# Graph network with experts on one core: one-hot rows two groups ahead, a tile's work in another order

## What is computed

```python
h = feats * rsqrt(deg_out)[:, None]
m = segment_sum(h[src], dst, num_segments=n) * rsqrt(deg_in)[:, None]
x = (m @ W_gc + b_gc) + (feats @ W_res + b_res)
logits = x @ Wg + bg
vals, idx = top_k(logits, 2)              # 64 experts, H = 512, gelu between w1 and w2
core = sum of the gated outputs of a node's two experts
y = x + core
y = (y - mean) * rsqrt(var + eps) * gamma + beta      # over the nodes
out = layernorm(feats + y)                # over the features
```

## Time and profile before

| | |
|---|---|
| three runs | 2939.91, 2944.16, 2950.51 us; median 2944.16 |
| profiled execution | 2947.52 us, its span 2945.7 us |
| busy, of the span | PE 2071.2 us (70%), PE weight loads 1711.2 (58%), DVE 1234.2 (42%), ACT 410.9 (14%), POOL 1890.4 (64%) |
| chain that ended last | POOL 40%, PE 25%, issue 19%, DVE 7%, DMA 4%, DVE's sequencer 3% |
| mean granted clock of PE | 0.83 of full speed |

### The profile page before, as it was taken

How to read it: one execution, slowest core, us unless ns; L and a number is a source line. 1 busy time by engine, 2 the same in 40 slices (tenths; PEclk the granted TensorE clock), 3 DMA queues, 4 the chain that set the end, 5 groups by cost and what they waited for, 6 DMA issues and landing times.

```text
span 2945.7 us, 44174 instructions
## 1 busy us (share of the span) xinstructions
PE 2071.2 (70%) x10250; PEld 1711.2 (58%) x10251; DVE 1234.2 (42%) x3115; ACT 410.9 (14%) x1358; POOL 1890.4 (64%) x1970
## 2 busy tenths in 40 slices
PE   8956555666656666666667777767766899999660
PEld 7944444454444555555556566556555788889650
DVE  8971121122223423444445455545563322222367
ACT  3010000000000000001001111111112223323113
POOL 0017777777777777777777777777735767777500
PEclk6556868778888878888888899989997999999885
DMA  8033333333333333333333333333324556656532
GB/s 297 0 102 106 106 106 106 105 107 108 108 107 107 110 108 109 109 109 110 109 108 111 111 109 112 111 110 112 111 60 130 173 163 204 197 194 203 189 104 87
DMA packets 205085, 362.81 MB, mean 123 GB/s; under 512 B 43080, under 2 KB 125814, under 8 KB 204814
## 3 DMA queue, kind: packets, MB, share of 16 engines
q0 software_dynamic: 93648, 230.69, 26.9%
q1 hardware_dynamic: 104058, 123.31, 13.0%
q10 hardware_dynamic: 7108, 6.43, 0.6%
HBM read 327.91 MB, written 57.52 MB: 131 GB/s over the span
## 4 chain that ended last, share of the span: by engine, by line
POOL 40%; PE 25%; issue 19%; DVE 7%; DMA 4%; DVEq 3%; ACT 1%; PEld 1%; POOLq 1%; ACTq 0%; SPq 0%; PEldq 0%
POOL ring L460 20%; POOL stage L460 18%; PE bank L1276 6%; PE bank L1270 6%; PE bank L1156 5%; PE bank L1136 3%; PE bank L1197 2%; PE bank L1261 1%; DMA ring<-nodes,slots 1%; DMA stage<-y 1%; PE bank L1176 1%; DVE stage L749 1%; POOL y L495 1%; DVE acc L1054 1%; PEld bank L1345 1%
## 5 line engine op out<-in xcount | busy, mean ns | idle before, releaser
L460 POOL DMA_INDIRECT ring<-table,ring_idx x792 | 751.4, 949 | 242.1 <-issue 239.9
L460 POOL DMA_INDIRECT stage<-table,ring_idx x771 | 731.3, 949 | 234.9 <-issue 232.9
L1156 PE MATMUL bank<-ring,hot 128*128 128x257 f32 x1056 | 306.9, 454 | 159.9 <-DMA ring<-table,ring_idx 145.1
L1156 PE MATMUL bank<-stage 128*128 128x257 f32 x1030 | 304.2, 460 | 138.8 <-DMA stage<-table,ring_idx 130.7
L1156 PEld LDWEIGHTS bank<-ring,hot 128*128 128x128 f32 x1056 | 238.6, 232 | 222.0 <-issue 142.8
L1156 PEld LDWEIGHTS bank<-stage 128*128 128x128 f32 x1030 | 236.1, 235 | 201.3 <-issue 127.3
L945 DVE TENSOR_TENSOR acc<-acc,bank 128x257 f32 x196 | 82.9, 423 | 567.5 <-PE bank L1156 529.2
L1156 PE MATMUL bank<-ring,stage 128*128 128x257 f32 x528 | 167.8, 487 | 109.2 <-DMA ring<-table,ring_idx 82.7
L1270 PEld LDWEIGHTS bank<-ring,stage 128*128 128x128 f32 x1984 | 235.0, 195 | 10.1 <-issue 3.9
L1270 PE MATMUL bank<-ring,stage 128*128 128x128 f32 x1984 | 238.1, 279 | 2.5 <-DVE ring L1001 1.1
L495 POOL DMA_INDIRECT y<-ring,slots x192 | 195.5, 1018 | 65.9 <-issue 47.6
(11 more groups left out here) (230 smaller groups left out, 2564.0 us busy)
## 6 DMA issues: line engine op xcount, KB each, us to landing
stage<-in_L_gnn_w_dram SPq DMA_DIRECT2D x128, 512.0 KB, 4.0
ring<-table,ring_idx POOLq DMA_INDIRECT x792, 2.8
y<-zeros SPq DMA_DIRECT2D x49, 256.0 KB, 2.2
stage<-y SPq DMA_DIRECT2D x14, 896.0 KB, 7.1
stage<-table,ring_idx POOLq DMA_INDIRECT x771
stage<-in_L_gnn_b_dram SPq DMA_DIRECT2D x64, 128.0 KB
nodes<-yS ACTq DMA_DIRECT2D x49, 128.0 KB
xs<-in_x_dram SPq DMA_DIRECT2D x1, 6144.0 KB
```

What stands on the lines that cost most here:

```text
L460: pool.indirect_dma_start(out=ring(q)[:, j, 0:D], out_offset=None, in_=table[:, :], in_offset=bass.IndirectOffsetOnAxis(ap=ring_idx[:, q, ...
L1156: last = pe.matmul(bank[:, 0:D + 1], hots[:, j, :], ring(q)[:, j, :], start=j == 0, stop=j == n - 1)
```

## The change

- `HOTS` is 3: a third buffer `hot_mid` beside the two of `hot`. VectorE makes the rows of the first two groups ahead of the loop, and in group g those of g+2.
- VectorE no longer makes the later group's rows first. It reads the code of g. With a second tile it makes that tile's rows (`rows_of`), then the later group's (`later`), then waits and adds (`sum_of`); third and further tiles go through the old loop. Without one it makes the later group's rows in the other arm of the branch.
- The first pass isn't written out for VectorE any more: PE raises `group_mm` by three ahead, so that all waits have one form.
- ScalarE copies `xs` to xS ahead of its wait for `deg`, and the copy of `acc` to mS now gives the signal.
- PE drops its wait for `deg`; `slots` goes first in a tile's work, `places` behind the transposes of mS and xS.

```diff
--- before.py
+++ after.py
@@ -26,7 +26,7 @@
 COLS = EB * P
 GCOLS = COLS // CPG
 RING = 6
-HOTS = 2
+HOTS = 3
 GROUPS = -(-EDGES // (P * CPG))
 STEPS = -(-GROUPS // RING)
 LASTQ = GROUPS - (STEPS - 1) * RING
@@ -102,7 +102,8 @@
         ring_idx = sb("ring_idx", [P, RING, CPG], I32)
 
         hot_low = sb("hot", [P, CPG, P])
-        hot = (hot_low[:, :, :], stage[:, high0:high0 + CPG * P].rearrange("p (j d) -> p j d", j=CPG))
+        hot_mid = sb("hot_mid", [P, CPG, P])
+        hot = (hot_low[:, :, :], stage[:, high0:high0 + CPG * P].rearrange("p (j d) -> p j d", j=CPG), hot_mid[:, :, :])
         slots = sb("slots", [P, 2, SC], I32)
         hotx = slots[:, :, :].rearrange("p a s -> p (a s)").bitcast(F32).rearrange("p (j d) -> p j d", j=CPG)
         loT = hot_low[:, :, :].rearrange("p j d -> p (j d)")[:, 0:COLS // 2].bitcast(BF16)
@@ -583,9 +584,9 @@
 
             def tick(i, behind):
                 if i is not None:
+                    act.activation(xS[:, :], xs[:, bass.ds(i, 1), :], ACT.Copy)
                     act.wait_ge(nd_deg, i + 1)
-                    act.activation(mS[:, :], acc[:, bass.ds(i, 1), 0:D], ACT.Copy)
-                    act.activation(xS[:, :], xs[:, bass.ds(i, 1), :], ACT.Copy).then_inc(nd_in, 1)
+                    act.activation(mS[:, :], acc[:, bass.ds(i, 1), 0:D], ACT.Copy).then_inc(nd_in, 1)
                     act.activation(tmp[:, bass.ds(i, 1)], deg[:, bass.ds(i, 1)], ACT.Sqrt).then_inc(nd_sqrt, 1)
 
                 def transposed_y(t):
@@ -828,30 +829,41 @@
             def one_hots(it, q, first=False):
 
                 g = it * RING + q
-                if not (first and q < HOTS):
-                    dve.wait_ge(group_mm, it * RING + (q - HOTS + 1))
+                if not first:
+                    dve.wait_ge(group_mm, it * RING + (q + 1))
                 dve.tensor_scalar(dstq[:, q % HOTS, :], dstT[:, bass.ds(g * CPG, CPG)], neg_base[:, bass.ds(g, 1)], None, ALU.add)
                 dve.drain()
                 dve.tensor_tensor(hot[q % HOTS], iota_ps.unsqueeze(1).to_broadcast([P, CPG, P]),
                                   dstq[:, q % HOTS, :].unsqueeze(2).to_broadcast([P, CPG, P]), ALU.is_equal).then_inc(hot_ready, 1)
 
-            def extras(g, c):
+            def extras(g, c, later):
 
                 first_tile, last_tile = field(dve, c, 0), field(dve, c, 1)
+
+                def rows_of(t):
+                    dve.drain()
+                    dve.tensor_scalar(dstx[:, :], dstT[:, bass.ds(g * CPG, CPG)], neg_tile[:, bass.ds(t, 1)], None, ALU.add)
+                    dve.drain()
+                    dve.tensor_tensor(hotx[:, :, :], iota_ps.unsqueeze(1).to_broadcast([P, CPG, P]),
+                                      dstx[:, :].unsqueeze(2).to_broadcast([P, CPG, P]), ALU.is_equal).then_inc(hotx_ready, 1)
+
+                def sum_of(t):
+                    dve.reg_add(extra, extra, 1)
+                    n = dve.snap(extra, min_val=1, max_val=GROUPS * NT)
+                    dve.wait_ge(groupx_mm, n)
+                    dve.tensor_tensor(acc[:, bass.ds(t, 1), :], acc[:, bass.ds(t, 1), :], banks[2][:, 0:D + 1], ALU.add)
                 with dve.If(last_tile > first_tile):
-                    with dve.Fori(first_tile + 1, last_tile + 1) as tile:
-                        t = a_tile(tile)
-                        dve.reg_add(extra, extra, 1)
-                        n = dve.snap(extra, min_val=1, max_val=GROUPS * NT)
-                        dve.drain()
-                        dve.tensor_scalar(dstx[:, :], dstT[:, bass.ds(g * CPG, CPG)], neg_tile[:, bass.ds(t, 1)], None, ALU.add)
-                        dve.drain()
-                        dve.tensor_tensor(hotx[:, :, :], iota_ps.unsqueeze(1).to_broadcast([P, CPG, P]),
-                                          dstx[:, :].unsqueeze(2).to_broadcast([P, CPG, P]), ALU.is_equal).then_inc(hotx_ready, 1)
-                        dve.drain()
-                        dve.wait_ge(groupx_mm, n)
-                        dve.tensor_tensor(acc[:, bass.ds(t, 1), :], acc[:, bass.ds(t, 1), :],
-                                          banks[2][:, 0:D + 1], ALU.add)
+                    second = a_tile(first_tile + 1)
+                    rows_of(second)
+                    later()
+                    sum_of(second)
+                    with dve.If(last_tile > first_tile + 1):
+                        with dve.Fori(first_tile + 2, last_tile + 1) as tile:
+                            t = a_tile(tile)
+                            rows_of(t)
+                            sum_of(t)
+                with dve.Else():
+                    later()
                 return first_tile
 
             def tick(i, behind):
@@ -927,28 +939,29 @@
                     dve.wait_ge(nd_sqrt, i + 1)
                     dve.reciprocal(rs[:, bass.ds(i, 1)], tmp[:, bass.ds(i, 1)]).then_inc(nd_recip, 1)
 
-            one_hots(0, 0, True)
+            for g in range(HOTS - 1):
+                one_hots(0, g, True)
             dve.sem_inc(nd_pick, DEPTH)
             dve.sem_inc(nd_sel, DEPTH)
 
-            def step(it, first, final=False):
+            def step(it, final=False):
                 for q in range(LASTQ if final else RING):
                     g = it * RING + q
-                    if q + 1 < (LASTQ if final else RING):
-                        one_hots(it, q + 1, first)
-                    elif not final:
-                        one_hots(it + 1, 0)
+                    def later(ahead=q + HOTS - 1):
+                        if ahead < (LASTQ if final else RING):
+                            one_hots(it, ahead)
+                        elif not final:
+                            one_hots(it + 1, ahead - RING)
                     c = group_code(dve, g)
-                    first_tile = extras(g, c)
-                    dve.drain()
-                    dve.wait_ge(group_mm, g + 1)
+                    first_tile = extras(g, c, later)
+                    dve.drain()
+                    dve.wait_ge(group_mm, g + (1 + HOTS))
                     dve.tensor_tensor(acc[:, bass.ds(first_tile, 1), :], acc[:, bass.ds(first_tile, 1), :],
                                       banks[q % 2][:, 0:D + 1], ALU.add).then_inc(acc_added, 1)
                     ticks_of_group(dve, c, tick)
-            step(0, True)
-            with dve.Fori(1, STEPS - 1) as it:
-                step(it, False)
-            step(STEPS - 1, False, True)
+            with dve.Fori(0, STEPS - 1) as it:
+                step(it)
+            step(STEPS - 1, True)
             last_ticks(dve, tick)
 
 
@@ -1157,16 +1170,6 @@
                 last.then_inc(done, 1)
 
             def tick(i, behind):
-                if i is not None:
-                    pe.wait_ge(nd_deg, i + 1)
-
-                def places(t):
-
-                    pe.wait_ge(nd_pick, t + (DEPTH + 1))
-                    pe.matmul(banks[2][:, 5 * EX:6 * EX], tri[:, :], picked[:, :], start=True, stop=False)
-                    pe.matmul(banks[2][:, 5 * EX:6 * EX], ones_b[:, :], taken[:, :], start=False, stop=True).then_inc(nd_rank, 1)
-                behind(2, places)
-
                 def slots(t):
 
                     pe.wait_ge(nd_sel, t + (DEPTH + 1))
@@ -1184,6 +1187,13 @@
                                             ident[:, :])
                     last.then_inc(nd_tr, 1)
 
+                def places(t):
+
+                    pe.wait_ge(nd_pick, t + (DEPTH + 1))
+                    pe.matmul(banks[2][:, 5 * EX:6 * EX], tri[:, :], picked[:, :], start=True, stop=False)
+                    pe.matmul(banks[2][:, 5 * EX:6 * EX], ones_b[:, :], taken[:, :], start=False, stop=True).then_inc(nd_rank, 1)
+                behind(2, places)
+
                 def transpose_y(t):
                     pe.wait_ge(nd_y, t + 1)
                     for k in range(DK):
@@ -1206,6 +1216,7 @@
                 behind(1, logits)
 
 
+            pe.sem_inc(group_mm, HOTS)
             pe.sem_inc(nd_rank, DEPTH)
             pe.sem_inc(nd_slot, DEPTH + 1)
             pe.sem_inc(out_ready, 1)
```

## The result

The changed kernel takes **2960.16 us** (median of 6 runs, 2954.15 to 2963.91); the kernel before takes 2946.44 (2939.91 to 2950.51) beside it. The ratio is 1.0052, 95% interval 1.0042 to 1.0063: slower by half a per cent, where no change was forecast (2945, range 2933 to 2955). A ratio here is not the quotient of the two medians; it differs from it by up to 0.001. The profiled execution took 2963.91 us, with a span of 2962.1.

A forecast was written before the change was run, and what follows sets the result against it. POOL's 1563 gathers without gaps (1958.9 us) bound the aggregation; only the backlog and last tiles behind them could change. Ten rounds +2.7, last groups -1.7, last tile -0.3 gave +0.7: 2945 us, no measurable change (0.70), range 2933 to 2955.

The forecast's parts named there:

- (3): Three one-hot buffers, two groups ahead: PE's multiplications end 0.5 us sooner, then wait for the second tile's rows; worth nothing.
- Rival B: PE stays at its full clock and the round is no longer: faster, 2933 us at the good ends; chance 0.13.
- (1): Second tile's rows ahead of the later group's on VectorE: 3.85 against 4.16 us, gain 0.3 us a round (0.1 to 0.6).
- (2): Group without a second tile: VectorE reads the code exposed, before its one-hots; loss 1.1 us a round (1.0 to 1.5).
- ten rounds: Rounds of two groups each, in the 21 groups from 172 to 193; seven at +0.6, three at -0.5: +2.7 us.
- (4): New tile order on PE and ScalarE: gain 0.2 us a tile, about 1.3 in three half-clock tiles of ten.
- (5): Last groups, from the gather stream's last deg to the last addition's end: 12.0 us instead of 13.6, -1.7 us.
- the backlog: How far multiplying and adding lag POOL's gathers: 12.5 us at group 172, 23.4 at the end; all the change can reach, with the last tiles.
- A: Rival: the exposed code reading, with a 0.5 us branch cost, makes the backlog grow; about +10, 2954 us; chance 0.13.
- C: Rival: VectorE's new forward branches stall as the back branch does, 3 us in 11 groups: +33, 2978 us; chance 0.04.
- The list of what to see: Expected profile: unchanged gathers, rows 3.9 us after the addition, PE waiting some 2 us, last addition ending at 2187 to 2199.

The follow-up runs named there:

- the batch at 3717 us: First batch of three kernels with throwaway products in PE's waits, where the kernel before itself took 3717 us; ratios to it 0.9989, 1.0254 and 1.0196.

## Why the prediction was wrong, step by step

**The failed step is (3), "this is worth nothing by itself".** It said rightly that PE "is late for the second tile's rows" next, and forecast the wait at some 2 us (it was 1.8 to 3.0, and 3.5 to 5.6 behind the back branch), but put no price on it. The price stood in the earlier trace rows: a second tile at 6.03 us instead of 3.75, behind an idle time of 5.74 us. No second tile of that stretch waited between 1.1 and 4.7 us, so whether 2 us is enough could not be read there; that up to 2.3 us a round stood at risk could. Rival B even named it, "new idle time of the kind ahead of which the clock fell", as a reason against a gain and not as a rival of its own that loses. With 12 of 15 second tiles at half clock after and 2 before, ten at 1.7 to 2.9 us each are about 18 us, which the product's part shows: 75.9 against 57.8. The third buffer alone, priced at 0, cost 0.32%.

The Trainium skill, page "TensorE: Matmul & The Clock Gate", section "HAM oscillation — how this bites in real kernels", describes this for waits on DMA transfers: a wait in every tile of a loop brings the clock down again and again, and half of the throttled time is lost. The traces agree on the loss: 42.3 - 4.7 = 37.6 us more half clock, halved 18.8, against the 18.1 us measured. The prediction did not weigh that page.

**(1) Second tile's rows first: right, a little better.** 4.16 to 3.67 us is 0.49 a round, within 0.1 to 0.6. The rows' part fell by 10.8 us in 14 rounds, 0.77 each, since behind the back branch VectorE is idle less too.
**(2) The exposed reading: right, at the low end.** +13.3 us in 14 rounds is 0.95 each over all, and 1.3 in the round shown, against 1.1 (1.0 to 1.5). The chain of waits after shows it, read, compare and branch from 2162.06 to 2163.26 with nothing beside them:

```profile
2162.06 0.32 DVEq L288
...
2162.70 0.04 DVEq L855
...
2163.00 0.14 issue
```

(1) and (2) together were forecast at +0.8 a round. Measured they nearly cancel: 13.3 - 10.8 = 2.5 us in 14 rounds, 0.2 each, from before to after, and 13.3 - 11.7 = 1.6 us between the two orders with filled waits. The 8.1 us of time between those two (2938.88 - 2930.80) equal the 8 us that ten rounds of +0.8 would give, but this is luck: their rounds differ by 6.9 us, of which 3.3 stand in the product's part.
**(4) The tile order: right on average in the trace, nothing in time.** The tile's part fell by 6.2 us in 14 rounds (forecast 5.3 in ten); by itself the tile order gave a ratio between 0.9995 and 1.0017. How much the tile loses to the clock changes with all else in the round, so the gain could not be counted on.
**(5) The last groups: wrong sign.** From the last deg (2196.35) to the end of the last addition (2211.16) are 14.8 us, before 13.6, forecast 12.0. The one-hots were ready as said; but the last tile's products ran at half clock:

```profile
2199.65 2.08 PE L1207 MATMUL bank<-wgc,tS 128*128 128x256 f32 x4 [0.96 <-ACT tS L598]
2201.52 1.91 PE L1207 MATMUL bank<-wres,tS 128*128 128x256 f32 x4
...
2204.22 0.23 DVE L923 TENSOR_TENSOR lg<-bank,bgb 128x64 f32<-128x64 f32 x1 [2.37 <-PE bank L1214]
```

**Only ten rounds were counted.** The sum took the backlog as equal to the earlier trace rows up to group 172. After, it is larger there already: that group's last gather and its addition are

```profile
1941.48 0.95 POOL L461 DMA_INDIRECT stage<-table,ring_idx  x1 [0.30 <-issue]
...
1965.68 0.42 DVE L959 TENSOR_TENSOR acc<-acc,bank 128x257 f32 x1 [0.26 <-issue]
```

23.7 us, where it was 12.5. The earlier rounds had little slack, and a longer round eats it sooner: 11.2 of the 21.0 us arose before the stretch that I had read. In the stretch itself and the last groups it is 9.8 us, where the sum had 1.
**A slip in the range.** The good ends of (1), (2) and (4) give seven rounds of about 0 and three of -0.9, with (5) and the last tile some -4.4 us, not the -6 stated. The forecast and the range don't hang on it.

**The rivals.** A was nearest in time (2954), with a wrong cause: of 148 jumps to the other arm 122 left the sequencer idle for 0.13 to 0.16 us and 26 for 0.43 to 0.51 (before, 22 of 148 for 0.46 to 0.49), so its branch cost of 0.5 in both groups did not show, and filling PE's wait took the loss away with the reading still exposed. B's mechanism is real, and worth more than I gave it, but needs the waits filled: then 2929 to 2931. C is refuted: VectorE's sequencer stands still for 2.7 us and more at the loop's back branch, some 30 times as before, and never behind the new forward branches. By the rule that the prediction takes from the Trainium skill's page "Runtime: NRT & Kernel Launch" (Instruction fetch mechanics), only a taken branch whose target lies outside the two pages held has to wait for a fetch. The trace agrees: the short jumps cost 0.51 us at most.
**The list of what to see** held for the gathers, the rows, the order and the waits. The last addition at 2211.16, beyond 2202, was to prove "A or C"; it proved neither: A's exposed reading is real, but nearly paid for by (1). The list had no entry for a cause that I hadn't priced.

What stays open: why the new VectorE order with two buffers, whose second tiles ran at the full clock in the one trace, spread over 32 us; and what share of the third buffer's 8 us comes through the tile's clock (31 us of half clock against 24) rather than the product's (15 against 5).

## What to carry to other kernels

When a change leaves the busiest chain alone but lets TensorE finish earlier and wait longer, price the wait by the slowest row of the same instruction in the trace, and look how long the engine had been idle ahead of it: in a kernel that alternates dense products and short waits, one longer wait can cost more than the chain saved. Test it cheaply: put throwaway products into the wait; if the time falls and the trace shows the clock kept, the clock was the loss. And where a backlog decides, count from the first round that has no slack, not from the one where the backlog shows.

## What the runs showed of the hardware that was not expected

- **Adding work to TensorE made kernels faster.** Ten throwaway products a tile (20 instructions in the trace, 1.50 + 1.06 us of PE) with the new tile order took the kernel before from 2943 to 2931 us, where that order alone took it nowhere.
- **Idle time and clock of the second tile's products, over the 13 traces outside the batch at 3717 us** (the 194 second tiles that start between 1850 and 2215 us): after an idle time under 2 us none of 128 was slowed; between 2 and 3 us 16 of 25; over 3 us 39 of 41. One just ahead of the stretch was slowed behind 1.98 us, so 2 us is no edge. A wait of 2.81 us was followed by 5.43 us of products in one round of after, and one of 2.88 by 3.75 in another: one row tells little, and the count tells more.
- **Half clock moves.** With the reading put ahead it left the second tile (42 to 14 us) and came up in the tile's work (17 to 48 us): a fill or a shorter wait at one place has to be judged over the whole round.
- **Reading one number to branch on costs VectorE about 1 us** when nothing lies beside it (2162.06 to 2163.00), and less when it is loaded into a register under other work: from the reciprocal to the next rows the idle time was then 0.55 us in place of 1.30.
